# Top-32 sparse cross-attention: searching folded score halves, and building the weights from signs on the scalar engine

## The chip, the cores and the metric

The kernel runs on one core of a Trainium2 chip. The metric is the device time of one execution, in microseconds (us). A step or a tile below is 128 rows of scores: two heads of one batch element, 64 queries each.

## What is computed

The program is a perceiver of four layers, each with a cross-attention, a self-attention and a feed-forward part, on x of shape 16 x 64 x 128 with a context of shape 16 x 1601 x 128. The change concerns one part, the cross-attention of the last layer:

```
scores = jnp.einsum('bhsd,bhnd->bhsn', Q, K) / SCALE            # 16 x 16 x 64 x 1601
topk_scores, topk_indices = jax.lax.top_k(scores, 32)
sparse_weights = jax.nn.softmax(topk_scores, axis=-1)
context = sum over the 32 of sparse_weights * V[topk_indices]
x = x + context @ Wo.T + bo
```

Of each row of 1601 scores only the 32 largest get a weight.

## The kernel before

The stage is `stage_l3_xattn` (L1376); its last call, `cross_attention` (L322) with `topk` set, holds nearly all of its work. A tile t has 128 rows (two heads of a batch element) by 1601 scores, there are 8 tiles for each of 16 batch elements and so 128 in all. The tiles are written out 16 at a time (`iteration`): the first and the last 16 stand alone, the six groups between run in a hardware loop (`Fori`). Semaphores alone order the engines; each engine's own order is the order of its code.

What each engine does with a tile:

- TensorE: `scores` (L458) multiplies four banks of PSUM full (8 passes of 512 or fewer columns), two tiles ahead (`AHEAD`, L341). Once per batch element `project` (L477) makes the keys in the same PSUM tile `psS`. `turn` (L495) transposes the weights in 13 chunks through `psT`, `values` (L508) multiplies them with the context into `psU` (26 passes), `turn_u` (L517) and `sums` (L523) bring the heads together.
- ScalarE: `copy_scores` (L594) moves the scores from PSUM to `SS`; `stationary` (L575) the keys, once per batch element; `exps_topk` computes EX = exp(SS - max) (L600) and, once the search is over, ER = exp(rest - max) (L602), in which the 32 largest are gone; `copy_weights` (L612) copies the transposed chunks, four at a time; `norm` (L608) divides by the sum.
- VectorE: `maxima` (L718) searches. It finds the eight largest values (`max`, L731 and L737) and strikes them out (`match_replace`, L735 and L738), four times, each over all 1601 columns. Between them it negates the maximum (L732), inverts the sum of weights (`inverse`, L783) and copies the head outputs (`copy_ut`, L787). Once per batch element `add` adds the result (L793) and the bias (L794) to x.
- GpSimd (POOL): P = EX - ER (L701), and once per batch element the spread queries (L691).

The search of a tile, as VectorE runs it:

```
link(dve.max(top[:, 0, :], SS[:, k, :]))
dve.tensor_scalar(m, top[:, 0, 0:1], -1.0, None, ALU.mult).then_inc(max_ready, 1)
if between:
    between()
link(dve.match_replace(rest[:, k, :], top[:, 0, :], SS[:, k, :], -3.0e38))
for r in range(1, 4):
    link(dve.max(top[:, r, :], rest[:, k, :]))
    last = dve.match_replace(rest[:, k, :], top[:, r, :], rest[:, k, :], -3.0e38)
```

The loads of the context (SP queue, L421 to L424) are issued when the values of the batch element that used the buffer are done.

Of the kernel before, what the change touches and what calls it, by code (L numbers as in the profile page):

```python
# [5 lines left out]
ALU = mybir.AluOpType  # L6
ACT = mybir.ActivationFunctionType
# [7 lines left out]
B, S, D = 16, 64, 128  # L15
NT = B * S // 128
K = 1601
KC = [(c * 128, min(128, K - c * 128)) for c in range((K + 127) // 128)]
KB = [(c * 512, min(512, K - c * 512)) for c in range((K + 511) // 512)]
H = 16  # L20
# [6 lines left out]
ONE = 1  # L27
# [74 lines left out]
def bc(ap, shape):  # L102
    return ap.to_broadcast(shape)
# [1269 lines left out]
                         None, 0.125, False)  # L1373


def stage_l3_xattn(c):  # L1376

    nc, d = c.nc, c.dram
    layernorm(c)
    with ExitStack() as st:  # L1380
        N = c.sb(st, "N3", [128, H, D])
        QT = c.sb(st, "QT", [128, B * S])
        WT = c.sb(st, "WT", [128, 3, D])
        bias = c.sb(st, "biases", [128, 3])
        with ExitStack() as s2:
# [11 lines left out]

            spread_bias(c, bias[:, 2:3], WT[:, 2, :], bo)
            project(c, QT, WT[:, 0, :], c.xnT, bias[:, 0:1], 8.0 ** -0.5)
        cross_attention(c, None, N, None, topk=(QT, WT[:, 1, :], bias[:, 1:2]))  # L1400


def spread_bias(c, col, w, bo):
# [1426 lines left out]
def add_aligned(c, hi_dram, lo_dram):  # L2830
# [4 lines left out]
    with ExitStack() as st:  # L2835
# [12 lines left out]
        with nc.Block() as block:  # L2848
# [68 lines left out]

STAGES = [stage_l0_xattn, stage_l0_attn, stage_l0_ffn, stage_l1_xattn, stage_l1_attn, stage_l1_ffn, stage_l2_xattn,
          stage_l2_attn, stage_l2_ffn, stage_l3_xattn, stage_l3_attn, stage_l3_ffn]


# [34 lines left out]
```

## Time and profile before

| what | value |
|---|---|
| median of 3 runs | 6238.86 us (6229.23 to 6241.07) |
| the profiled execution's own time | 6232.65 us |
| its span | 6230.8 us |
| mean granted TensorE clock, share of full | 0.801 |
| busy: TensorE, VectorE, ScalarE, GpSimd | 4076.0, 4351.5, 2261.9, 937.9 us |
| the stage that is changed, from its first projection to its last add | 3667.55 to 5787.18 us of the span |

Times in the rows below are microseconds from the start of the span; PE is TensorE's matmul side, DVE is VectorE, ACT is ScalarE, POOL is GpSimd. In a row of a group, "x384" is the number of instructions, then comes their busy time and the mean of one in nanoseconds, then the idle time before them and what ended it. In a row of the timeline the first number is the start, the second how long the row's instructions took together; brackets hold the idle time before them and its releaser.

### The profile page before, as it was taken

The numbers are of one execution on the slowest core, as the hardware profiler recorded it, in microseconds if no ns is written. First come the engines' busy times: TensorE is split into PE (matmuls) and PEld (weight loads), VectorE is DVE, ScalarE is ACT, GpSimd is POOL, SyncE is SP. The second block draws the span as 40 slices with busy tenths as digits, with TensorE's granted clock in tenths as the row PEclk, the third lists the DMA queues.
The fourth block names the chain that finished last, engine by engine and source line by source line (L and its number), as shares of the span: only waits on it lengthen the run. The fifth ranks groups of instructions, "written<-read, shape, count | busy, mean of one in ns | idle before, by whom it ended". The sixth has DMA issues, their size and how long they took to land. (4 is left out here: it accounts for less than half of the span.)

```text
span 6230.8 us, 69499 instructions
## 1 busy us (share of the span) xinstructions
PE 4076.0 (65%) x23936; PEld 3283.5 (53%) x23936; DVE 4351.5 (70%) x5857; ACT 2261.9 (36%) x3210; POOL 937.9 (15%) x537
## 2 busy tenths in 40 slices
PE   4511556259999856799997546666666666666475
PEld 3201523148888834688886324454444545445464
DVE  3486334667777642577775369999999999999343
ACT  0000012126666532466664214444444444444111
POOL 1200010011111010212110102222222222222100
PEclk7755567679999978999998778887888887878676
DMA  6643300011111000111100000000000000000000
GB/s 209 154 109 81 91 2 0 4 46 33 33 33 33 12 6 27 47 37 33 38 28 13 4 24 11 11 11 22 11 11 11 11 22 11 11 11 1 15 0 12
DMA packets 199464, 198.78 MB, mean 32 GB/s; under 512 B 10908, under 2 KB 182124, under 8 KB 199164
## 3 DMA queue, kind: packets, MB, share of 16 engines
q1 hardware_dynamic: 179132, 156.79, 9.1%
q10 hardware_dynamic: 20032, 38.13, 2.1%
q8 instruction: 172, 2.82, 0.2%
q14 instruction: 128, 1.05, 0.1%
HBM read 161.47 MB, written 33.42 MB: 31 GB/s over the span
## 5 line engine op out<-in xcount | busy, mean ns | idle before, releaser
L1127 PEld LDWEIGHTS psU<-ctxN,ST 128*128 128x128 f32 x6656 | 859.5, 192 | 71.0 <-issue 9.5
L1127 PE MATMUL psU<-ctxN,ST 128*128 128x129 f32 x6656 | 869.1, 276 | 4.4 <-issue 4.4
L495 PE MATMUL psT<-ident,P 128*128 128x128 f32 (+1 forms) x1664 | 366.3, 376 | 600.9 <-POOL P L701 564.2
L737 DVE MAX8 top<-rest 128x8 f32<-128x1601 f32 x384 | 702.3, 1829 | 37.3 <-DVE rest L738 2.7
L738 DVE MATCH_REPLACE8 rest<-top,rest 128x1601 f32<-128x1601 f32 x384 | 695.4, 1811 | 0.0
L701 POOL TENSOR_TENSOR P<-EX,ER 128x1601 f32<-128x1601 f32 x128 | 457.7, 3576 | 1463.9 <-ACT ER L602 1463.9
L495 PEld LDWEIGHTS psT<-ident,P 128*128 128x128 f32 (+1 forms) x1664 | 275.5, 195 | 643.6 <-issue 420.6
L1213 ACT ACTIVATE ST<-ST 128x512 f32<-128x512 f32 (+1 forms) x832 | 519.8, 626 | 219.4 <-DVE ST L1316 216.6
L1316 DVE TENSOR_TENSOR ST<-ST,psB 128x512 f32<-128x512 f32 (+1 forms) x832 | 561.8, 678 | 13.4 <-PE psB L1146 13.4
L1302 DVE TENSOR_TENSOR psA<-psA,ST 128x512 f32<-128x512 f32 x640 | 445.5, 696 | 131.3 <-ACT ST L1205 68.8
L458 PE MATMUL psS<-KT,stat 128*128 128x512 f32 (+1 forms) x1024 | 438.9, 577 | 88.2 <-ACT KT L575 73.9
L508 PE MATMUL psU<-ctxN,PT 128*128 128x129 f32 (+1 forms) x3328 | 480.5, 304 | 0.0
L508 PEld LDWEIGHTS psU<-ctxN,PT 128*128 128x128 f32 (+1 forms) x3328 | 471.2, 223 | 0.0
L612 ACT ACTIVATE PT<-psT 128x512 f32<-128x512 f32 (+1 forms) x512 | 260.2, 516 | 492.1 <-PE psT L495 492.0
L1115 PE MATMUL psS<-statL,ctxH 128*128 128x512 f32 x832 | 395.1, 475 | 6.2 <-ACT ST L1205 2.7
L458 PEld LDWEIGHTS psS<-KT,stat 128*128 128x128 f32 x1024 | 210.1, 216 | 315.7 <-issue 236.1
L602 ACT ACTIVATE ER<-rest,mx 128x1601 f32<-128x1601 f32 x128 | 208.8, 1631 | 417.8 <-DVE rest L738 417.8
L1205 ACT ACTIVATE ST<-psS,key_bias 128x512 f32<-128x512 f32 (+1 forms) x416 | 284.1, 683 | 146.3 <-PE psS L1115 144.5
L1115 PE MATMUL psS<-statH,ctxH 128*128 128x512 f32 x832 | 331.6, 399 | 0.0
L1115 PE MATMUL psS<-statH,ctxL 128*128 128x512 f32 x832 | 328.6, 395 | 0.0
L1208 ACT ACTIVATE ST<-psS 128x512 f32<-128x512 f32 (+1 forms) x416 | 246.6, 593 | 158.9 <-PE psS L1115 156.2
L594 ACT ACTIVATE SS<-psS 128x1601 f32<-128x1601 f32 x128 | 192.1, 1501 | 207.3 <-PE psS L458 207.0
(420 smaller groups left out, 6690.5 us busy)
## 6 DMA issues: line engine op xcount, KB each, us to landing
ctxT<-ctxT_scratch SPq DMA_DIRECT2D x64, 800.5 KB, 4.3
ctxN<-in_ctx SPq DMA_DIRECT2D x64, 768.0 KB
ctxT_scratch<-ctx_trn ACTq DMA_DIRECT2D x16, 800.5 KB, 7.4
ctx_nat<-in_ctx SPq DMA_DIRECT2D x16, 768.0 KB
dist_scratch<-dd ACTq DMA_DIRECT2D x8, 800.5 KB, 5.4
cur<-cost_scratch SPq DMA_DIRECT2D x16, 400.2 KB, 6.7
left<-cost_scratch SPq DMA_DIRECT2D x16, 400.2 KB, 7.8
step_scratch<-nxt ACTq DMA_DIRECT2D x8, 800.5 KB, 3.4
```

The source lines that it names most:

```text
L458: last = pe.matmul(psS[:, o:o + w], stat[:, j, 2 * n:2 * n + 2, :], KT[:, j, o:o + w], start=True, stop=True)
L495: last = pe.transpose(psT[0:w, q % 2, (k % 4) * 128:(k % 4) * 128 + 128], P[:, t % 2, o:o + w], c.ident[:])
L508: last = pe.matmul(psU[:, 0:VW], PT[0:w, t % 2, k, :], ctxN[0:w, t // TB, k, 0:VW], start=(k == 0), stop=(k == len(KC) - 1))
L701: pool.tensor_tensor(P[:, t % 2, :], EX[:], ER[:], ALU.subtract).then_inc(p_ready, 1)
L737: link(dve.max(top[:, r, :], rest[:, k, :]))
L738: last = dve.match_replace(rest[:, k, :], top[:, r, :], rest[:, k, :], -3.0e38)
L1115: last = pe.matmul(psS[:, i % RING, :], x[:, u // 2 % 2, o:o + 128], q[:, p % 2, heads, queries], start=(n_pass == 0), stop=(n_pass == 2))
L1127: last = pe.matmul(psU[:, q, 0:D + 1], ST[0:n, i % SLOTS, q * 128:q * 128 + 128], ctxN[0:n, j, k, 0:D + 1], start=(k == 0 and q % 2 == 0), ...
L1205: act.activation(ST[0:n, i % SLOTS, :], psS[0:n, i % RING, :], ACT.Identity, bias=key_bias[0:n, col:col + 1]).then_inc(copied, 1)
L1213: act.activation(ST[0:n, i % SLOTS, :], ST[0:n, i % SLOTS, :], ACT.Exp).then_inc(exp_done, 1)
L1302: dve.tensor_tensor(psA[:], psA[:], cell, ALU.max).then_inc(folded, 1)
L1316: dve.tensor_tensor(cell, cell, psB[0:n, :], ALU.subtract).then_inc(shifted, 1)
```

## The change

`stage_l3_xattn` calls a new function, `topk_cross_attention`, in place of `cross_attention` with `topk` set. All 128 tiles are written out, with no hardware loop.

- Search: each row is folded into pairs. Columns 0 to 800, read from PSUM, and columns 801 to 1600, read from `SS` with one column of padding behind them, give an elementwise maximum and an elementwise minimum of 801 columns each, side by side in `pairs`. Two rounds of `max` and `match_replace` run over the maxima alone, the third over both halves, and the fourth is a `max` only: its eighth value is the 32nd score, the edge.
- Weights: ScalarE takes Sign(edge - score) over the row and over the 32 found values, with their sums. GpSimd and VectorE work out from the sums how many scores equal the edge and what share each of them gets. ScalarE turns the signs into a huge value above the edge, the share at it and nothing below (Relu), GpSimd clamps to 1 and multiplies with EX.
- Order: TensorE computes the scores one tile ahead of the search, and the projection stands right before the scores of a batch element's first tile. Transposes and values belong to the tile two steps back. The head outputs are copied by ScalarE, sums are made for two batch elements at once, and the bias is added once, by GpSimd, before the tiles.

The diff, cut to what matters here:

```diff
--- before.py
+++ after.py
+def topk_cross_attention(c, N, QT, WkT, bk):
+
+    nc = c.nc
+    NC = len(KC)
+    TB = H // 2
+    T = B * TB
+    HALF = (K + 1) // 2
+    KP = 2 * HALF
+    LOW = -3.0e38
+    STEEP = 1.0e28
+    TOPK = 32
+    LISTS = 7
...
+        SS = c.sb(st, "SS", [128, 3, KP])
+        pairs = c.sb(st, "pairs", [128, 2, KP])
+        EX = c.sb(st, "EX", [128, 2, K])
...
+                for j in range(3):
+                    pool.memset(SS[:, j, K:KP], LOW).then_inc(filled, 1)
+                pool.tensor_tensor(c.x[:], c.x[:], bc(c.bias_row[:].rearrange("p (a d) -> p a d", a=1), [128, NT, D]),
+                                   ALU.add).then_inc(filled, 1)
...
+                    if b >= 2:
+                        sp.wait_ge(u_ready, TB * (b - 1) + ONE)
...
+                def project(b):
+                    pe.wait_ge(loaded[b % 2], 48 * (b // 2 + 1) + ONE)
+                    if b:
+                        pe.wait_ge(copied, TB * b + ONE)
+                        pe.wait_ge(folded, 2 * TB * b + ONE)
+                    for o, w in KB:
+                        last = pe.matmul(psS[:, o:o + w], WkT, ctxT[:, b % 2, o:o + w], start=True, stop=True)
+                    last.then_inc(kp_ready, 1)
+
+                def scores(t):
+                    b, n = t // TB, t % TB
+                    if n == 0:
+                        project(b)
+                        pe.wait_ge(kt_ready, b + 1 + ONE)
+                        pe.wait_ge(stat_ready, b + 1 + ONE)
+                    else:
+                        pe.wait_ge(copied, t + ONE)
+                        pe.wait_ge(folded, 2 * t + ONE)
+                    for o, w in KB:
+                        last = pe.matmul(psS[:, o:o + w], stat[:, b % 2, 2 * n:2 * n + 2, :], KT[:, b % 2, o:o + w],
+                                         start=True, stop=True)
+                    last.then_inc(scored, 1)
...
+                scores(0)
+                for s in range(T + 2):
+                    if s + 1 < T:
+                        scores(s + 1)
+                    t = s - 2
+                    if t >= 1:
+                        turn_u(t - 1)
+                        if t % (2 * TB) == 0:
+                            sums(t // (2 * TB) - 1)
+                    if t >= 0:
+                        turn(t, 0)
+                        turn(t, 1)
+                        values(t, 0)
+                        turn(t, 2)
+                        values(t, 1)
+                        turn(t, 3)
+                        values(t, 2)
+                        values(t, 3)
+                turn_u(T - 1)
+                sums(NT - 1)
...
+                def keys(b):
+                    act.wait_ge(kp_ready, b + 1 + ONE)
+                    if b >= 2:
+                        act.wait_ge(scored, TB * (b - 1) + ONE)
+                    act.activation(KT[:, b % 2, :], psS[:, 0:K], ACT.Identity, bias=bk).then_inc(kt_ready, 1)
+                def copy_scores(t):
+                    if t % TB == 0:
+                        keys(t // TB)
+                    act.wait_ge(scored, t + 1 + ONE)
+                    if t >= 3:
+                        act.wait_ge(sided, t - 2 + ONE)
+                        act.wait_ge(exp_done, t - 2 + ONE)
+                    act.activation(SS[:, t % 3, 0:K], psS[:, 0:K], ACT.Copy).then_inc(copied, 1)
...
+                    act.activation(mneg[:, t % 2:t % 2 + 1], top[:, t % 2, 0:1], ACT.Copy, scale=-1.0
+                                   ).then_inc(max_ready, 1)
...
+                    act.activation(EX[:, t % 2, :], SS[:, t % 3, 0:K], ACT.Exp, bias=mneg[:, t % 2:t % 2 + 1]
+                                   ).then_inc(exp_done, 1)
...
+                def count_sides(t):
+                    j = t % 2
+                    edge = top[:, j, TOPK - 1:TOPK]
+                    act.wait_ge(listed, LISTS * (t + 1) + ONE)
+                    if t:
+                        act.wait_ge(marked, t + ONE)
+                    if t >= 2:
+                        act.wait_ge(spanned, 2 * (t - 1) + ONE)
+                        act.wait_ge(share_ready, t - 1 + ONE)
+                    act.activation(sides[:], SS[:, t % 3, 0:K], ACT.Sign, scale=-1.0, bias=edge,
+                                   accum_out=below[:, j:j + 1]).then_inc(sided, 1)
+                    if t:
+                        act.wait_ge(counted, t + ONE)
+                    act.activation(listed_sides[:], top[:, j, :], ACT.Sign, scale=-1.0, bias=edge,
+                                   accum_out=above[:, j:j + 1]).then_inc(counted, 1)
...
+                    act.wait_ge(share_ready, t + 1 + ONE)
+                    act.wait_ge(sided, t + 1 + ONE)
+                    if t >= 2:
+                        act.wait_ge(turned, 4 * (t - 1) + ONE)
+                    act.activation(P[:, j, :], sides[:], ACT.Relu, scale=-STEEP, bias=share[:, j:j + 1]
+                                   ).then_inc(marked, 1)
...
+                copy_scores(0)
+                for s in range(T + 2):
+                    if 0 <= s - 1 < T:
+                        count_sides(s - 1)
+                    if s + 1 < T:
+                        copy_scores(s + 1)
+                    if 0 <= s - 1 < T:
+                        mark(s - 1)
+                    if s < T:
+                        negate(s)
+                        exps(s)
+                    if s >= 3:
+                        copy_ut(s - 3)
+                    if s >= 2:
+                        for q in range(4):
+                            copy_weights(s - 2, q)
+                        norm(s - 2)
...
+                def equal_span(t):
+                    j = t % 2
+                    pool.wait_ge(counted, t + 1 + ONE)
+                    pool.wait_ge(sided, t + 1 + ONE)
+                    if t >= 2:
+                        pool.wait_ge(span_inverted, t - 1 + ONE)
+                    pool.tensor_scalar(span[:, j:j + 1], above[:, j:j + 1], 2.0, below[:, j:j + 1], ALU.mult, ALU.subtract
+                                       ).then_inc(spanned, 1)
+                    pool.wait_ge(spanned, 2 * t + 1 + ONE)
+                    pool.tensor_scalar(span[:, j:j + 1], span[:, j:j + 1], float(K), None, ALU.add
+                                       ).then_inc(spanned, 1)
+
+                def weigh(t):
+                    j = t % 2
+                    pool.wait_ge(span_inverted, t + 1 + ONE)
+                    if t >= 2:
+                        pool.wait_ge(marked, t - 1 + ONE)
+                    pool.tensor_scalar(share[:, j:j + 1], above[:, j:j + 1], float(TOPK), inv_span[:, j:j + 1],
+                                       ALU.add, ALU.mult).then_inc(share_ready, 1)
+                    pool.wait_ge(marked, t + 1 + ONE)
+                    pool.tensor_scalar(P[:, j, :], P[:, j, :], 1.0, None, ALU.min).then_inc(clamped, 1)
+                    pool.wait_ge(clamped, t + 1 + ONE)
+                    pool.wait_ge(exp_done, t + 1 + ONE)
+                    pool.tensor_tensor(P[:, j, :], P[:, j, :], EX[:, j, :], ALU.mult).then_inc(p_ready, 1)
...
+                def fold(t, low):
+                    j = t % 2
+                    lo, hi = psS[:, 0:HALF], SS[:, t % 3, HALF:KP]
+                    dve.wait_ge(copied, t + 1 + ONE)
+                    if t >= 2:
+                        dve.wait_ge(listed, LISTS * (t - 1) + ONE)
+                    if low:
+                        dve.tensor_tensor(pairs[:, j, HALF:KP], lo, hi, ALU.min).then_inc(folded, 1)
+                    else:
+                        dve.tensor_tensor(pairs[:, j, 0:HALF], lo, hi, ALU.max).then_inc(folded, 1)
...
+                    dve.max(top[:, j, 8 * n:8 * n + 8], pairs[:, j, 0:width]).then_inc(listed, 1)
...
+                    dve.match_replace(pairs[:, j, 0:width], top[:, j, 8 * n:8 * n + 8], pairs[:, j, 0:width], LOW
+                                      ).then_inc(listed, 1)
...
+                def invert_span(t):
+                    j = t % 2
+                    dve.wait_ge(spanned, 2 * t + 2 + ONE)
+                    if t >= 2:
+                        dve.wait_ge(share_ready, t - 1 + ONE)
+                    dve.reciprocal(inv_span[:, j:j + 1], span[:, j:j + 1]).then_inc(span_inverted, 1)
+
+                def inverse(t):
+                    dve.wait_ge(u_ready, t + 1 + ONE)
+                    if t >= 2:
+                        dve.wait_ge(us_ready, t - 1 + ONE)
+                    dve.reciprocal(li[:, t % 2:t % 2 + 1], psU[:, D:D + 1]).then_inc(li_ready, 1)
+
+                def add(p):
+                    dve.wait_ge(y_ready, p + 1 + ONE)
+                    dve.tensor_tensor(c.x[:, p, :], c.x[:, p, :], psZ[:, 128:256], ALU.add).then_inc(y_added, 1)
+
+                fold(0, False)
+                fold(0, True)
+                for s in range(T + 2):
+                    if s < T:
+                        find(s, 0, HALF)
+                    if s >= 3:
+                        inverse(s - 3)
+                    if s < T:
+                        drop(s, 0, HALF)
+                        find(s, 1, HALF)
+                    if 0 <= s - 1 < T:
+                        invert_span(s - 1)
+                    if s < T:
+                        drop(s, 1, HALF)
+                        find(s, 2, KP)
+                    if s - 2 > 0 and (s - 2) % (2 * TB) == 0 and s - 2 < T:
+                        add((s - 2) // (2 * TB) - 1)
+                    if s + 1 < T:
+                        fold(s + 1, False)
+                    if s < T:
+                        drop(s, 2, KP)
+                    if s + 1 < T:
+                        fold(s + 1, True)
+                    if s < T:
+                        find(s, 3, KP)
+                inverse(T - 1)
+                add(NT - 1)
...
 
             spread_bias(c, bias[:, 2:3], WT[:, 2, :], bo)
             project(c, QT, WT[:, 0, :], c.xnT, bias[:, 0:1], 8.0 ** -0.5)
-        cross_attention(c, None, N, None, topk=(QT, WT[:, 1, :], bias[:, 1:2]))
+        topk_cross_attention(c, N, QT, WT[:, 1, :], bias[:, 1:2])
 
 
 def spread_bias(c, col, w, bo):
```

## Rows read from the trace of the kernel before

**Rows 1.** Timeline, PE and DVE: the first projection and the last add of the stage.
```profile
3667.55 5.81 PE L477 MATMUL psS<-ctxT,WT 128*128 128x512 f32 x8 [11.20 <-DMA ctxN<-in_ctx]
...
5786.89 0.29 DVE L794 TENSOR_TENSOR x<-x,bias_row 64x128 f32<-64x128 f32 x1
```

**Rows 2.** Windows of the stage: busy time of each engine, granted clock, DMA share, GB/s.
```profile
3800.00:4056.00 256.00, 164.73 (x845) 127.32 (x845) 247.59 (x245) 113.20 (x131) 61.00 (x18) 0.83 0.04 13
```

**Rows 3.** Groups of instructions in the stage, VectorE.
```profile
L737 DVE MAX8 top<-rest 128x8 f32<-128x1601 f32 x384 | 702.3, 1829 | 37.3 <-DVE rest L738 2.7 <-DVE rest L735 2.7
L738 DVE MATCH_REPLACE8 rest<-top,rest 128x1601 f32<-128x1601 f32 x384 | 695.4, 1811 | 0.0
...
L738 DVE MATCH_VALUE_LOAD rest<-top,rest 128x8 f32 x384 | 35.4, 92 | 35.2 <-DVE top L737 2.7
```

**Rows 4.** Timeline, VectorE: the start of a tile's small work, two tiles of the written-out end.
```profile
5740.01 0.15 DVE L732 TENSOR_SCALAR mx<-top 128x1 f32<-128x1 f32 x1
...
5755.38 0.15 DVE L732 TENSOR_SCALAR mx<-top 128x1 f32<-128x1 f32 x1
```

**Rows 5.** Groups by form, VectorE: a two-input operation from PSUM and from SBUF.
```profile
L1302 DVE TENSOR_TENSOR psA<-psA,ST 128x512 f32<-128x512 f32 x640 | 445.5, 696 | 131.3 <-ACT ST L1205 68.8 <-ACT ST L1208 58.6
...
L2688 DVE TENSOR_TENSOR a<-cur,left 128x1601 f32<-128x1601 f32 x8 | 14.6, 1829 | 0.8
```

**Rows 6.** Timeline, POOL and DVE: the two adds to x beside a POOL operation.
```profile
4773.44 3.56 POOL L701 TENSOR_TENSOR P<-EX,ER 128x1601 f32<-128x1601 f32 x1 [13.93 <-ACT ER L602]
...
4773.90 0.29 DVE L793 TENSOR_TENSOR x<-x,psZ 64x128 f32 x1
4774.30 2.85 DVE L794 TENSOR_TENSOR x<-x,bias_row 64x128 f32 x1
```

**Rows 7.** Groups by form, GpSimd.
```profile
L701 POOL TENSOR_TENSOR P<-EX,ER 128x1601 f32<-128x1601 f32 x128 | 457.7, 3576 | 1463.9 <-ACT ER L602 1463.9
...
L1244 POOL CAST ctxH<-ctxM 128x1601 fp32r<-128x1601 f32 x32 | 48.9, 1529 | 1027.1 <-DVE ctxM L1275 1027.1
...
L1255 POOL CAST statH<-statM 128x512 fp32r<-128x512 f32 x64 | 40.5, 633 | 107.6 <-DVE statM L1283 107.6
...
L1478 POOL TENSOR_SCALAR_AFFINE_SELECT flag<-flag 128x1 f32<-128x1 f32 x64 | 11.8, 185 | 4.4
```

**Rows 8.** Groups by form, ScalarE.
```profile
L612 ACT ACTIVATE PT<-psT 128x512 f32<-128x512 f32 x384 | 225.2, 597 | 384.2 <-PE psT L495 384.1
...
L600 ACT ACTIVATE EX<-SS,mx 128x1601 f32<-128x1601 f32 x128 | 207.4, 1621 | 1.2 <-issue 1.1
L594 ACT ACTIVATE SS<-psS 128x1601 f32<-128x1601 f32 x128 | 192.1, 1501 | 207.3 <-PE psS L458 207.0
...
L608 ACT ACTIVATE U<-psU,li 128x128 f32<-128x128 f32 x128 | 47.0, 367 | 74.5 <-DVE li L783 74.0 <-issue 0.5
...
L575 ACT ACTIVATE KT<-psS,biases 128x1601 f32<-128x1601 f32 x16 | 25.4, 1590 | 44.4 <-PE psS L477 44.4
```

**Rows 9.** Timeline, PE: two tiles and a projection between them.
```profile
4797.14 2.91 PE L495 MATMUL psT<-ident,P 128*128 128x128 f32 x12 [5.57 <-POOL P L701]
4799.85 1.93 PE L508 MATMUL psU<-ctxN,PT 128*128 128x129 f32 x8
...
4804.57 2.91 PE L477 MATMUL psS<-ctxT,WT 128*128 128x512 f32 x8
4811.68 5.54 PE L458 MATMUL psS<-KT,stat 128*128 128x512 f32 x8 [4.20 <-ACT KT L575]
...
4820.79 2.17 PE L508 MATMUL psU<-ctxN,PT 128*128 128x129 f32 x18
```

**Rows 10.** Windows, PE alone, of that stretch: busy, granted clock, DMA share, GB/s.
```profile
4798.00:4802.00 4.00, 4.00 (x20) 0.50 0.00 0
4803.00:4807.00 4.00, 4.00 (x21) 0.98 0.00 0
```

**Rows 11.** Groups by form, ScalarE: the table load of the stage.
```profile
L600 ACT ACT_TABLE_LOAD x1 | 1.3, 1283 | 0.0
```

158 lines of the change are left out of this document (added).

## The prediction

> **What bounds the kernel now.** I read four views. First the timeline at the stage's two ends [rows 1]: from the first projection at 3667.55 to the last add's end at 5787.18 it takes 2119.6 us, 16.56 us for each of 128 tiles. Then the windows [rows 2]: in 256 us VectorE is busy 247.6, TensorE 164.7, ScalarE 113.2, POOL 61.0. VectorE is the bound. Then the groups [rows 3]: each of a tile's four rounds costs 1.83 (max) + 0.09 (value load) + 1.81 (replace), 14.9 us together. Last the timeline of VectorE [rows 4]: where the tiles are written out, one takes 15.37, so all else costs 0.45 there. The loop's bounds, the projection and the adds to x make up the difference to 16.56.
>
> **The change, part by part.**
>
> *VectorE's own work.* A two-input operation costs 0.696 for 512 columns with one input in PSUM and 1.829 for 1601 in SBUF [rows 5], so 1.04 ns a column, and 1.00 for a fold of 801. For max and replace over 801 columns there is no row. Bounds: no shorter than now (1.83, 1.81), or shorter by 800 x 1.04 = 0.83. I take the second, because their present times are those of the 1.829 row, which does follow its columns. A tile is then: max 2 x 1.00 + 2 x 1.83, replace 2 x (0.98 + 0.09) + 1.90, folds 2 x 1.00, two small inversions at 0.15 [rows 4], gaps 0.3: 12.3 us, three less than 15.37. The fourth replace is gone, the copy of head outputs has moved to ScalarE. The bias adds of 2.85 [rows 6], one per batch element, leave too; their one successor on POOL, ahead of the tiles, costs 1024/1601 of 3.58 [rows 7], 2.3, on the path.
>
> *What queues behind what.* Three engines now wait for each other inside a step. Take step s from the end of values of tile s-3. VectorE inverts the sum of s-3 (in its queue behind the first max of s). ScalarE waits for it with its whole queue: norm 0.37, Sign over 1601 columns 1.63 (as the Exp with a bias, [rows 8]), Sign over 32 columns about 0.3, and two sums out; no row has such a sum, I bound it by 0 and 0.3 and take 0.2. That is 2.6 us. Meanwhile TensorE, whose scores of s+1 stand behind the values of s-3, needs 2.91 for them at full clock [rows 9] (the projection has the same eight passes). So copying the scores starts at 3.15. The Sign work is covered by TensorE, with 0.5 to spare.
>
> *The small hand-over.* After the signs: POOL, POOL, VectorE (reciprocal), POOL, then ScalarE's mark. No row has POOL's tensor_scalar on one column. Bounds: 0.185 (a select on one column) and 0.633 (a cast of 512) [rows 7]. I take 0.25, the one-column row plus a little for the pointers. With 0.1 a crossing, the share is there at about 4.0 and the score copy ends at 4.3, so 0.3 is left before it costs. VectorE's reciprocal stands between two rounds of the search and VectorE waits there 1.3 us per step: 12.3 + 1.3 = 13.7 is VectorE's ring, counted in inversion again.
>
> *The ring through ScalarE and TensorE.* scores 2.91; score copy 1.50, mark 1.63, negate 0.2, Exp 1.62, head copy 0.3, first weight copy 0.60, less 0.1 of overlap for each of four [rows 8]: 5.4; hand-overs 0.35 (estimate: 0.1 each, 0.15 more after a matmul; ends 0.1 and 0.5); then TensorE's tail behind the first weight copy: values, transposes, values, transpose, values, values. The tail depends on the clock. After its pause TensorE needs 1.93 for eight value passes and 2.91 for twelve transposes; later 18 passes take 2.17 [rows 9]. The granted clock is 0.50 in 4798 to 4802 and 0.98 in 4803 to 4807 [rows 10], that is 1.2 and 2.4 GHz, and it fell after TensorE had stood idle 5.57. The tail is 7.5 all slow, 3.75 all fast. In the new order TensorE does two groups of transposes and then stands about 5 us until the weight copy, like before, so I let it be slow for 3.9, the stretch at 0.50 that [rows 10] show: 3.9 + 0.48 x 3.75 = 5.7. Sum: 2.91 + 5.4 + 0.35 + 5.7 = 14.4, and 0.4 because one tile in some has slow scores (5.54 against 2.91, [rows 9]): **14.8 a tile**. That is over VectorE's 13.7, so VectorE waits at the inversion.
>
> *POOL.* Clamp between 1.53 (one-input cast) and 3.58 (two-input) [rows 7], I take 1.6, and the product 3.58. The mark ends 5.9 into the ring, so weights are there at 11.2. They are needed only behind the next scores: 3 us of cover, gone only if the ring fell below 11.
>
> *Per batch element.* The projection, before it hidden two tiles ahead, stands in the ring: 2.91 + keys 1.59 + hand-overs 0.35, and partly slow scores behind the short pause: 5.9 (ends 4.8 and 8), 15 times. For two batch elements at once 32 sums passes come ahead of the transposes: 3.9 at the value passes' fast rate, 7.7 slow; partly beside the Exp; I take 6 (ends 0 and 10), 7 times. Context loads wait on values of the batch before, with six tiles of cover; the SP queue loses nothing.
>
> *Sum.* 127 x 14.8 = 1880; 15 x 5.9 = 89; 7 x 6 = 42; filling until the first tile's values end 50; last sums 5: 2066 against 2119.6, that is -54, and +2 for the bias on POOL: -51. The profiled execution's own time is 6232.65, so 6181; the median lies 6.2 above it: **6188**.
>
> **Rivals.** A difference of 0.2% (12 us) is about what a measurement of this kernel can tell from none.
>
> 1. *The clock stays up and VectorE is the bound.* TensorE's order keeps it busier than before (its work per tile falls little, the tile gets shorter). With the tail at 3.75 the ring is 12.9 and VectorE's 13.7 rules: 127 x 13.7 + 15 x 5 + 55 = 1870, that is 5992. For it: only about 5 us of pause. Against: a pause of 5.57 was enough for 0.50 [rows 9, 10]. Chance 0.17.
> 2. *POOL's small operations are slow* (the slower side). Place: the three one-column operations in front of the mark. They decide from about 0.35 us each; at 0.63 it is 3 x 0.38 - 0.3 = 0.84 a tile, +107: 6295. For it: POOL's 0.633 for 512 columns and 1.529 for 1601 leave 0.21 without any column, and pointer operands come on top. Against: the select of 0.185. Chance 0.24.
> 3. *Table loads.* The stage now loads a table once, 1.28 us [rows 11]. If Sign and Relu don't lie with Exp, each tile gets two: 1.28 in the ring and 0.8 beyond the cover at the Sign, 2.1 x 127 = 267: 6455. For it: no row shows Sign beside Exp. Against: Copy, Identity and Exp alternate all through the stage with one load. Chance 0.07. The Trainium skill ("ScalarE: Activation LUTs", "Table sets: the hidden batching unit") says that one set is active at a time and that relu, copy, identity and abs come in every set; it doesn't name sign there. Its "What ACT_TABLE_LOAD costs" adds a drain of about 1.38 to each switch, by which this case would be an estimated 350 us dearer still.
> 4. *POOL holds the folds.* The add with both inputs in SBUF took 2.85 beside POOL's product, until that ended, and the one with an input in PSUM 0.29 in the same stretch [rows 6]. A fold has one input in PSUM, like the short one. If it were held like the long one, up to 2.5 each, VectorE's ring is about 17.2: +2.4 x 127, 6490. Chance 0.04. The Trainium skill ("SBUF — State Buffer", "Who interferes with whom") has two SBUF inputs, not one, as the condition; this trace agrees, 2.85 against 0.29.
> 5. *Max and replace don't shorten with their columns:* VectorE's ring 13.7 + 3.3 = 17.0, some 6470. Chance 0.02.
>
> **How the numbers follow.** The forecast has 0.46; its own range, with tail, batch and sum costs at their ends, is 6090 to 6270, so 0.38 of it is faster, 0.05 within 0.2% and 0.03 slower. Rival 1 is faster. Rival 2 begins at no change: 0.03 faster, 0.05 the same, 0.16 slower. Rivals 3 to 5 are slower. Faster 0.58, same 0.10, slower 0.32. The range 6030 to 6320 leaves out rivals 3 to 5 (0.13) and the far part of rival 1 (0.07).
>
> **What would show it.** Right: VectorE idle ahead of the inversion of the value sum, released by TensorE; a folded max near 1.00; folds near 1.00; tiles 14 to 15.5 apart and about 6 more at every eighth; a granted clock of 0.50 at the first value passes. Rival 1: no such wait and 13.7 apart. Rival 2: a one-column POOL operation of over 0.35, and mark released by POOL. Rival 3: 250 table loads. Rival 4: folds with a spread up to 3.5. The forecast is wrong if the score copy doesn't wait for the scores, or if the weight copies aren't what TensorE's values wait for.

## The result and the profile of the changed kernel

The changed kernel takes 6053.96 us (median of 4 runs, 6051.49 to 6061.95) against 6234.05 us (6228.55 to 6241.07) on the same chip: ratio 0.9711, 95% interval 0.9696 to 0.9725, so 180 us less. The prediction said 6188, 51 us less than the median of before that was known then (6238.86). The profiled execution took 6051.49, its span is 6049.8, and its mean granted clock 0.810 (0.801 before).

The ends of the stage, in the timelines of TensorE and VectorE, where before stand [rows 1]:

```profile
3668.20 4.79 PE L1463 MATMUL psS<-ctxT,WT 128*128 128x512 f32 x8 [13.24 <-DMA ctxN<-in_ctx]
...
5598.50 0.29 DVE L1730 TENSOR_TENSOR x<-x,psZ 128x128 f32<-128x128 f32 x1 [5.03 <-PE psZ L1513]
```

5598.79 - 3668.20 = 1930.6 us, 189.0 less than before. Behind the stage 451.0 us are left, 443.6 before: the other 7.4 us were given back there, in code that didn't change. So the question is one stage, and there one tile.

The groups of the stage (x128 is once a tile). Columns: number of instructions, busy us, mean ns, idle us before them and what ended it.

```profile
L1669 POOL TENSOR_SCALAR P<-P 128x1601 f32<-128x1601 f32 x128 | 552.1, 4314 | 333.7 <-ACT P L1591 333.7
L1672 POOL TENSOR_TENSOR P<-P,EX 128x1601 f32<-128x1601 f32 x128 | 457.8, 3577 | 10.7
...
L1578 ACT ACTIVATE sides<-SS,top 128x1601 f32<-128x1601 f32 x128 | 207.6, 1622 | 5.6 <-DVE top L1707 5.4
L1591 ACT ACTIVATE P<-sides,share 128x1601 f32<-128x1601 f32 x128 | 207.5, 1621 | 2.6 <-POOL share L1666 2.6
...
L1655 POOL TENSOR_SCALAR span<-above,below 128x1 f32<-128x1 f32 x128 | 39.2, 306 | 392.1 <-ACT listed_sides L1582 392.1
L1666 POOL TENSOR_SCALAR share<-above,inv_span 128x1 f32<-128x1 f32 x128 | 34.2, 268 | 38.5 <-DVE inv_span L1720 38.5
L1658 POOL TENSOR_SCALAR span<-span 128x1 f32<-128x1 f32 x128 | 29.2, 228 | 10.5
...
L1578 ACT ACTIVATION_READ_ACCUMULATOR sides<-SS,top 128x1 f32 x128 | 24.3, 190 | 0.0
...
L1726 DVE RECIPROCAL li<-psU 128x1 f32<-128x1 f32 x128 | 21.4, 168 | 222.4 <-PE psU L1497 222.4
L1720 DVE RECIPROCAL inv_span<-span 128x1 f32<-128x1 f32 x128 | 21.0, 164 | 140.0 <-POOL span L1658 140.0
L1566 ACT ACT_TABLE_LOAD x1 | 1.3, 1283 | 0.0
```

VectorE, by form:

```profile
L1707 DVE MAX8 top<-pairs 128x8 f32<-128x1602 f32 x256 | 467.2, 1825 | 4.4
L1707 DVE MAX8 top<-pairs 128x8 f32<-128x801 f32 x256 | 252.6, 987 | 4.4
L1712 DVE MATCH_REPLACE8 pairs<-top,pairs 128x801 f32<-128x801 f32 x256 | 250.4, 978 | 0.0
L1712 DVE MATCH_REPLACE8 pairs<-top,pairs 128x1602 f32<-128x1602 f32 x128 | 231.9, 1811 | 0.0
```

Max and replace follow their columns, the folds (L1691, L1693) take 0.98, Sign and Relu come without a table load of their own, POOL's one-column operations take 0.23 to 0.31, and VectorE now waits in two places of a plain tile, for the value sum and for the span. (A plain tile is any but the first two of a batch element, those in which head sums are made, and those right behind these.)

One plain tile, the timeline of all engines from one inversion of a value sum to the next (start, duration; brackets hold the idle time before it and its releaser):

```profile
4686.70 2.91 PE L1476 MATMUL psS<-KT,stat 128*128 128x512 f32 x8
4686.90 0.17 DVE L1726 RECIPROCAL li<-psU 128x1 f32<-128x1 f32 x1 [1.50 <-PE psU L1497]
...
4687.37 1.62 ACT L1578 ACTIVATE sides<-SS,top 128x1601 f32<-128x1601 f32 x1
...
4689.65 1.51 ACT L1553 ACTIVATE SS<-psS 128x1601 f32<-128x1601 f32 x1 [0.26 <-PE psS L1476]
...
4690.14 0.16 DVE L1720 RECIPROCAL inv_span<-span 128x1 f32<-128x1 f32 x1 [1.08 <-POOL span L1658]
...
4691.05 1.62 ACT L1591 ACTIVATE P<-sides,share 128x1601 f32<-128x1601 f32 x1
4691.29 1.83 DVE L1707 MAX8 top<-pairs 128x8 f32<-128x1602 f32 x1
...
4692.79 1.63 ACT L1566 ACTIVATE EX<-SS,mneg 128x1601 f32<-128x1601 f32 x1
4693.04 0.97 DVE L1693 TENSOR_TENSOR pairs<-psS,SS 128x801 f32<-128x801 f32 x1
...
4694.49 1.07 ACT L1600 ACTIVATE PT<-psT 128x512 f32<-128x512 f32 x2
4695.22 1.52 PE L1497 MATMUL psU<-ctxN,PT 128*128 128x129 f32 x8 [4.62 <-ACT PT L1600]
...
4697.38 1.93 PE L1497 MATMUL psU<-ctxN,PT 128*128 128x129 f32 x8
...
4699.27 1.28 PE L1497 MATMUL psU<-ctxN,PT 128*128 128x129 f32 x10
...
4700.39 1.88 PE L1476 MATMUL psS<-KT,stat 128*128 128x512 f32 x4
4700.59 0.17 DVE L1726 RECIPROCAL li<-psU 128x1 f32<-128x1 f32 x1 [1.25 <-PE psU L1497]
```

This is how a ring is read: each bracket names who was late. The scores take 2.91; the score copy starts 0.04 behind them; ScalarE's row of work runs without a gap from 4689.65 until TensorE's values start at 4695.22, 5.57; and TensorE's tail lasts until the next scores at 4700.39, 5.17. Together 13.69 us. VectorE's wait at the end of this tile is the 1.25 us of 4700.59, the same at every plain tile looked at; the 1.50 at 4686.90 ends the tile before, the one behind the head sums. The starts of L1726 through the whole stage show 13.69 at plain tiles, 19.6 at a batch element's first tile with 14.3 behind it, and 20.2 where the head sums are made, with 13.9 behind it. 127 x 13.69 = 1739, 15 x 6.5 = 98, 7 x 6.75 = 47, and some 47 for the first tile and the last sums: 1931.

### The profile page after: what moved, and what is told of

The parts are those of the page before. It is cut to its first block and busy times, and to the rows that moved or that the text cites. A ratio compares the mean times of both kernels' runs of the same rounds, so it can differ in the third digit from the quotient of the medians.

```text
span 6049.8 us, 68883 instructions
## 1 busy us (share of the span) xinstructions
PE 4024.5 (67%) x23680; PEld 3292.2 (54%) x23680; DVE 3812.9 (63%) x5705; ACT 2530.6 (42%) x3978; POOL 1595.2 (26%) x1053
## 5 line engine op out<-in xcount | busy, mean ns | idle before, releaser
L1497 PE MATMUL psU<-ctxN,PT 128*128 128x129 f32 (+1 forms) x3328 | 622.8, 352 | 565.9 <-ACT PT L1600 565.9
L1497 PEld LDWEIGHTS psU<-ctxN,PT 128*128 128x128 f32 (+1 forms) x3328 | 581.0, 262 | 592.6 <-issue 588.4
L1707 DVE MAX8 top<-pairs 128x8 f32<-128x801 f32 (+1 forms) x512 | 709.2, 1406 | 8.9
L1669 POOL TENSOR_SCALAR P<-P 128x1601 f32<-128x1601 f32 x128 | 552.1, 4314 | 333.7 <-ACT P L1591 333.7
L1712 DVE MATCH_REPLACE8 pairs<-top,pairs 128x801 f32<-128x801 f32 (+1 forms) x384 | 482.2, 1256 | 0.0
L1672 POOL TENSOR_TENSOR P<-P,EX 128x1601 f32<-128x1601 f32 x128 | 457.8, 3577 | 10.7
L1476 PE MATMUL psS<-KT,stat 128*128 128x512 f32 (+1 forms) x1024 | 379.9, 513 | 42.2 <-ACT KT L1544 27.0
L1244 POOL CAST ctxH<-ctxM 128x1601 fp32r<-128x1601 f32 x32 | 49.0, 1531 | 1028.7 <-DVE ctxM L1275 1028.7
L1476 PEld LDWEIGHTS psS<-KT,stat 128*128 128x128 f32 x1024 | 185.7, 191 | 232.8 <-issue 203.6
L1487 PE MATMUL psT<-ident,P 128*128 128x128 f32 (+1 forms) x1664 | 308.0, 320 | 0.4 <-POOL P L1672 0.4
```

What stands on the lines that cost most here:

```text
L1476: last = pe.matmul(psS[:, o:o + w], stat[:, b % 2, 2 * n:2 * n + 2, :], KT[:, b % 2, o:o + w], start=True, stop=True)
L1487: last = pe.transpose(psT[0:w, q % 2, (k % 4) * 128:(k % 4) * 128 + 128], P[:, t % 2, o:o + w], c.ident[:])
L1497: last = pe.matmul(psU[:, 0:D + 1], PT[0:w, t % 2, k, :], ctxN[0:w, t // TB % 2, k, 0:D + 1], start=(k == 0), stop=(k == NC - 1))
L1669: pool.tensor_scalar(P[:, j, :], P[:, j, :], 1.0, None, ALU.min).then_inc(clamped, 1)
L1672: pool.tensor_tensor(P[:, j, :], P[:, j, :], EX[:, j, :], ALU.mult).then_inc(p_ready, 1)
L1707: dve.max(top[:, j, 8 * n:8 * n + 8], pairs[:, j, 0:width]).then_inc(listed, 1)
```

## The experiments

Two theories stood against each other. **The ring theory**: scores, ScalarE and TensorE's tail close the tile, and VectorE waits. **The VectorE theory**: the prediction had VectorE's own ring, with its wait at the span, at 13.7 a tile, which is just the spacing found; by it the rest of the prediction's ring would be an error, and each microsecond of VectorE's work would count. All runs are timed against the kernel before on their chip (medians 6229.74, 6236.82 and 6235.01 for the three groups of runs).

**VectorE's work reduced.** The third round and the last maximum over the 801 maxima only (the minima are never searched, so a pair with two of the 32 scores gives one):

```diff
-                        find(s, 2, KP)
+                        find(s, 2, HALF)
...
-                        drop(s, 2, KP)
+                        drop(s, 2, HALF)
...
-                        find(s, 3, KP)
+                        find(s, 3, HALF)
```

> The third round and the last max search only the 801 maxima, so that the weights of some rows are not those of the reference. VectorE has 2.5 us less to do per tile. Theory A (a ring through ScalarE and TensorE sets the pace: scores, score copy, mark, Exp, weight copies, values, with 1.5 us in which VectorE waits at the inversion): nothing to gain, 6045 to 6060 us against 6054 of the changed kernel, and VectorE's wait at the inversion grows from 1.5 to about 4 us. Theory B (VectorE's own work sets the pace): 127 x 2.5 = 317 less, about 5740.

6057.21 us, ratio 0.9722 (0.9701 to 0.9743): no change. The work went out and the wait took its place, as this kernel's group of the stage shows:

```profile
L1726 DVE RECIPROCAL li<-psU 128x1 f32<-128x1 f32 x128 | 21.6, 168 | 519.1 <-PE psU L1497 518.7
```

518.7 - 222.4 = 296 us, 2.3 a tile. VectorE doesn't set the tile.

**The ring lengthened.** The mark is made twice, the first time into a tile that nobody reads:

```diff
+        again = c.sb(st, "again", [128, 2, K])
...
+                    act.activation(again[:, j, :], sides[:], ACT.Relu, scale=-STEEP, bias=share[:, j:j + 1])
                     act.activation(P[:, j, :], sides[:], ACT.Relu, scale=-STEEP, bias=share[:, j:j + 1]
```

> The mark (Relu) is computed twice, once into a spare tile: 1.53 us more on ScalarE per tile, nothing on VectorE, TensorE or POOL. Theory A (ring through ScalarE and TensorE): the ring grows by 1.53 and more of the values fall into a low clock, 127 x 1.53 = 194 or more: 6250 to 6320 us. Theory B (VectorE's work is the bound, ScalarE has slack): no change, 6054.

6258.4 us, ratio 1.0048 (1.0031 to 1.0066): 204 us more, where 127 x 1.62 = 206 is what the second mark takes on ScalarE. In the profiled execution (6272.95, the longest of the five) the stage is 230 us longer and what lies behind it 8 us shorter. So ScalarE's large passes count in full, and TensorE's tail adds to them: its pause is 6.13 us in place of 4.62, the tail behind it takes 4.9 to 6.5 us in place of 5.17, and the spacing is no longer even (14.9 to 16.6, 1.9 more in the mean).

**VectorE's work increased.** All rounds over 1602 columns:

```diff
-                        dve.wait_ge(folded, 2 * t + 1 + ONE)
+                        dve.wait_ge(folded, 2 * t + 2 + ONE)
...
-                        find(s, 0, HALF)
+                        find(s, 0, KP)
...
-                        drop(s, 0, HALF)
-                        find(s, 1, HALF)
+                        drop(s, 0, KP)
+                        find(s, 1, KP)
...
-                        drop(s, 1, HALF)
+                        drop(s, 1, KP)
```

> All rounds of the search run over the full 1602 columns, as before the change, but with the new order and the sign weights. VectorE's ring grows by 3.3 us from 12.2 to 15.5 per tile. Theory A: 1.5 of it is covered by the wait at the inversion, the rest of 1.8 costs 127 x 1.8 = 230: about 6285 to 6310. So the halves would be worth 230 us, not 420. Theory B (VectorE has no slack): 127 x 3.3 = 420, about 6475.

6145.92 us, ratio 0.9861 (0.9841 to 0.9881): 92 us more, far below what was expected. The expectation counted only the wait at the value sum as cover. This kernel's groups show that the wait at the span went too:

```profile
L1724 DVE RECIPROCAL li<-psU 128x1 f32<-128x1 f32 x125 | 19.7, 157 | 48.2 <-PE psU L1497 48.2
L1718 DVE RECIPROCAL inv_span<-span 128x1 f32<-128x1 f32 x127 | 18.4, 145 | 0.0
```

Cover was 1.25 + 1.08 = 2.33 of the 3.33 us added, which leaves 1.0. Plain tiles take 14.57 to 14.63 and about every third 15.1, against 13.69, and in the profiled executions the stage is 115 us longer than the changed kernel's. Behind it, in code that didn't change, 23 us less are left, so that the whole is only some 95 longer. So VectorE bounds the tile only with some 2.3 us more work, and its own work of a plain tile is 14.6 - 3.33 = 11.3 us. Seen from the other side, searching half of the columns in the first two rounds brings 92 of the change's 180 us; the rest is the new order, the missing fourth replacement and the weights from signs together, which no run takes apart.

**The two moves that shorten the ring.** ScalarE's negation and exponential go behind the second weight copy, so that TensorE's tail starts while the exponential runs; VectorE inverts the span after its second replacement:

```diff
-                    if s < T:
-                        negate(s)
-                        exps(s)
                     if s >= 3:
                         copy_ut(s - 3)
                     if s >= 2:
-                        for q in range(4):
-                            copy_weights(s - 2, q)
+                        copy_weights(s - 2, 0)
+                        copy_weights(s - 2, 1)
+                    if s < T:
+                        negate(s)
+                        exps(s)
+                    if s >= 2:
+                        copy_weights(s - 2, 2)
+                        copy_weights(s - 2, 3)
                         norm(s - 2)
...
-                    if 0 <= s - 1 < T:
-                        invert_span(s - 1)
-                    if s < T:
                         drop(s, 1, HALF)
+                    if 0 <= s - 1 < T:
+                        invert_span(s - 1)
+                    if s < T:
                         find(s, 2, KP)
```

> Negation and Exp move behind the second weight copy on ScalarE, into the time in which it waits for the next transposes, and VectorE's inversion of the span moves one instruction back. Theory A: the ring loses 1.8 us, VectorE's ring of about 12 becomes the bound; 1.0 to 1.5 us less a tile, 130 to 190 in all: 5865 to 5925 us. Theory B (VectorE bound before the move): only the wait of 1.08 at the span goes, 127 x 1 = 130, and the wait at the inversion stays as it is. If neither holds, no change.

5778.2 us (5761.67 to 5799.22), ratio 0.9265 (0.9235 to 0.9295): 276 us less than the changed kernel, far more than the 130 to 190 that were expected. Then each move alone, with the clamp left out as a third:

> Of the two moves that were tried together (278 us less than the changed kernel), this is the first alone: ScalarE's negation and exponential (0.19 + 1.63 us of a tile) are issued after the first two of the four weight copies instead of ahead of them. Theory of the ring (a tile of 13.69 us is closed by scores, ScalarE and TensorE's values): the first values start about 1.8 us earlier in each tile, VectorE's wait for them (1.50 us at the inversion of the value sum) goes, and its wait for the span (1.08 us) stays, so a plain tile takes 13.69 - 1.50 = 12.2 us at best: up to 190 us less than the changed kernel's 6054, ratio to the kernel before 0.94 to 0.95. If the exponential's later end holds the weights of the tile after next instead, only some 40 us less, ratio 0.965. Theory that VectorE's own work bounds the tile: nothing, ratio 0.971.

> The second move alone: VectorE inverts the span (the row's divisor) after its second replacement instead of ahead of it. The wait of 1.08 us for POOL's span goes from VectorE. Theory of the ring through ScalarE and TensorE: the time that VectorE wins is waited out at the inversion of the value sum (1.50 us becomes about 2.6), and nothing is won: 6054 within 10, ratio 0.971. Theory that VectorE with its waits sets the tile: 1.08 us x 127 = 137 us less, ratio 0.949.

The first alone: 5834.05 us, ratio 0.9355 (0.9340 to 0.9371), 220 us less. Its fastest and most common plain tiles take 12.33 us, near the 12.2 expected. 195 us of the 223 between the two profiled spans lie in the stage; the other 27, which the expectation didn't have, lie behind it, in unchanged code, where the profile shows a granted clock of 0.72 and 0.79 in the first two stretches of 200 us against 0.65 and 0.72. The second alone: 6057.65 us, ratio 0.9714 (0.9698 to 0.9731), nothing. The wait only changes its place:

```profile
4688.75 0.16 DVE L1720 RECIPROCAL inv_span<-span 128x1 f32<-128x1 f32 x1
...
4699.20 0.17 DVE L1726 RECIPROCAL li<-psU 128x1 f32<-128x1 f32 x1 [2.33 <-PE psU L1497]
```

It pays only behind the first: once the ring is short enough, the span's 1.0 us is on the path (12.33 - 1.0 = 11.3, and with both together the fastest plain tiles take 11.28). 0 + 220 is less than 276: the gains don't add, because the bound passes from one ring to the other. The stages of the profiled executions say the same: 0 and 195 us alone, 263 together. Both kernels with the late exponential leave TensorE a pause of 2.87 us in many tiles, and the tail behind such a pause took 3.85, 5.0, 5.17 or 6.45 us; what decides which, these runs don't show.

**POOL's clamp left out.** Scores above the edge then weigh 1e28 against the share of those at it:

```diff
-                    pool.tensor_scalar(P[:, j, :], P[:, j, :], 1.0, None, ALU.min).then_inc(clamped, 1)
-                    pool.wait_ge(clamped, t + 1 + ONE)
```

> Leaves out POOL's minimum with 1 over the marks (4.31 us of a tile); the weights of the scores above the edge then come out too large, everything else is computed. POOL's work of a tile falls from 4.31 + 3.58 + 2.34 + 0.8 = 11.0 to 6.7 us. Theory of the ring: POOL ends its product long before the transposes want it, so nothing changes: 6054 within 10, ratio 0.971. Rival: POOL's clamp holds the product and with it the transposes, or its traffic slows VectorE's reads of SBUF: up to 4.3 x 127 us less on the path, or some 0.1 to 0.5 us of a tile (13 to 60 us) from faster searches.

6052.68 us, ratio 0.9704 (0.9687 to 0.9720): nothing. The clamp's 4.31 us a tile are off the path and don't slow VectorE either: the folds take 0.98 in both kernels, beside the clamp in the changed one and, for the first fold of a tile, beside the product here.

**TensorE kept busy in its pause.**

```diff
                         turn(t, 1)
+                        for _ in range(15):
+                            pe.matmul(psU[:, 256:384], c.ident[:], c.ident[:], start=True, stop=True)
                         values(t, 0)
```

> Adds 15 matmuls of 128x128 of the identity, into a part of the value bank that is unused then, in TensorE's pause of 4.6 us between the transposes of the second half and the values of the first. Nothing else is changed. Theory of the ring: the granted clock stays at its upper level through the tail of values and transposes (5.17 us of which 3.4 us are at the lower one), the tail takes about 1.3 us less of a tile, of which the waits that are left let 0.6 to 1.1 through: some 80 us less than the changed kernel, 5975, ratio 0.959 (0.950 to 0.965). Rival one: the clock's fall in the tail doesn't come from the pause, and the dummies only stand in the way: 0 to 40 us more. Rival two (VectorE bounds): nothing.

5846.43 us, ratio 0.9372 (0.9356 to 0.9388): 208 us less, where 80 were expected. The expectation put the 15 matmuls at 1.8 us; the trace shows them as 30 passes that take 3.51. The pause shrinks from 4.62 to between 1.3 and 2.0 us and the tail to 3.52:

```profile
4509.95 3.51 PE L1530 MATMUL psU<-ident 128*128 128x128 f32 x30
4515.02 1.13 PE L1497 MATMUL psU<-ctxN,PT 128*128 128x129 f32 x8 [1.55 <-ACT PT L1602]
...
4516.42 1.06 PE L1497 MATMUL psU<-ctxN,PT 128*128 128x129 f32 x8
...
4517.42 1.28 PE L1497 MATMUL psU<-ctxN,PT 128*128 128x129 f32 x10
4518.54 2.91 PE L1463 MATMUL psS<-ctxT,WT 128*128 128x512 f32 x8
```

The windows of TensorE alone say why; first this kernel's tails, then those of the changed kernel (first a batch element's first tile, behind the projection; then the plain tile above). Columns: us, busy, granted clock, DMA share, GB/s.

```profile
4502.70:4506.20 3.50, 3.50 (x31) 1.00 0.00 0
4515.00:4518.50 3.50, 3.48 (x31) 1.00 0.00 0
```

```profile
4502.10:4503.90 1.80, 1.80 (x8) 0.50 0.00 0
4503.90:4506.40 2.50, 2.50 (x13) 0.50 0.00 0
```

```profile
4695.20:4696.50 1.30, 1.28 (x8) 0.73 0.00 0
4696.50:4697.40 0.90, 0.90 (x7) 0.50 0.00 0
4697.40:4699.20 1.80, 1.80 (x10) 0.50 0.00 0
4699.30:4700.30 1.00, 1.00 (x12) 1.00 0.00 0
```

A value of 1.00 is 2.4 GHz and 0.50 is 1.2 GHz. In the plain tile the clock is still up when TensorE resumes after 4.62 us without work, falls to 0.50 during the first eight value passes and is up again for the last ten. With work in the pause it stays up. The changed kernel has the same case of its own: where head sums are made TensorE has 32 more passes to do and stands idle for only 0.34 us before the values, and that tail takes 3.52 too. With the 15 matmuls the tail gets 1.65 us shorter; VectorE's wait for the value sum (1.25) goes, and VectorE's own work with its wait at the span (1.0) then sets the tile: 12.33, 1.36 less. My expectation of 0.6 to 1.1 took too little of this. A batch element's first two tiles won more (16.3 and 12.35 instead of 19.6 and 14.3), the sums' tiles lost (21.5 instead of 20.2). The stage is 181.5 us shorter, and 22 us more were won behind it.

**A smaller dose.** 4 matmuls in place of 15:

```diff
-                        for _ in range(15):
+                        for _ in range(4):
```

> As the run with 15 matmuls in TensorE's pause, which took 208 us from the changed kernel, with 4 instead of 15 (some 0.5 us instead of 1.8 us of the 4.6 us pause). The theory that the tail is slow because TensorE idles ahead of it, with the pause nearly as long as before: most of the gain goes, 6040 (6000 to 6060), ratio 0.969. Rival, that any work at that place holds the clock: about the same gain as with 15, 5850, ratio 0.937.

6033.25 us, ratio 0.9683 (0.9652 to 0.9713). Plain tiles still take 13.69. The 4 matmuls take 1.06 us, the pause is 3.72, and the tail behind it, from the first values to the next scores, is 5.17 as before:

```profile
4698.92 1.71 PE L1497 MATMUL psU<-ctxN,PT 128*128 128x129 f32 x8 [3.72 <-ACT PT L1602]
...
4704.09 2.91 PE L1476 MATMUL psS<-KT,stat 128*128 128x512 f32 x8
```

So that some work stands at that place isn't enough. The interval overlaps that of the changed kernel; the stage is 23 us shorter in the profiled executions, nearly all of it at the first two tiles of a batch element and around the sums.

**The best version.** Both moves and the loop of matmuls with `range(9)`; and then this kernel without them in the sums' tiles and with `add` behind `find(s, 3, KP)`, whose diff against the one with 9 is:

```diff
-                        for _ in range(9):
+                        for _ in range(9 if t % (2 * TB) or not t else 0):
...
-                    if s - 2 > 0 and (s - 2) % (2 * TB) == 0 and s - 2 < T:
-                        add((s - 2) // (2 * TB) - 1)
...
                         find(s, 3, KP)
+                    if s - 2 > 0 and (s - 2) % (2 * TB) == 0 and s - 2 < T:
+                        add((s - 2) // (2 * TB) - 1)
```

> Both moves (5778 together) and 9 matmuls of the identity in the pause that is left to TensorE (2.87 us of a tile). Theory: with both moves VectorE's own work of 11.28 us bounds a plain tile wherever the tail runs at the upper clock, and the tiles of 11.6 to 13.6 us are those with a slow tail; held up, all plain tiles take 11.28 us. 127 x 11.28 = 1433, + 15 x 4.3 for the batch elements' first tiles, + 7 x 8 for the sums (as with the 15 matmuls) = 1554 against the 1614 us of both moves: 5718, ratio 0.917 (0.910 to 0.924). Rival: the clock is up often enough already and the 9 matmuls (1.05 us) only push the values back: 0 to 40 us more than both moves, ratio 0.927 to 0.934.

> As the last run, but without the 9 matmuls in the seven tiles in which the head sums are made, and with VectorE's addition of a sum after the last maximum of its tile instead of ahead of the first fold. Theory: VectorE's wait for the sum (7.44 us of each such tile with the 15 matmuls) and the push of 1.05 us go, the tile keeps a hold-up of 2 to 4 us because the transposes start 4.6 us late behind the sum's 32 matmuls: 7 x 3 to 7 x 5 = 20 to 35 us less than the run before it. Rival: the hold-up comes through the transposes alone and the addition waits beside it: 0 to 8 us less.

5726.33 us, ratio 0.9186 (0.9159 to 0.9214), 8 us off the expectation, most plain tiles at 11.29, the tile behind the sums at 13.0; and 5706.46 us, ratio 0.9163 (0.9128 to 0.9197). Between the two the intervals overlap, so the last 20 us aren't settled; the spacing shows 1.0 to 1.2 us less at six of the seven sums' tiles (16.1 to 16.4 for 17.3 to 17.6), some 7 us, and more of the batch elements' first tiles at 14.9 instead of 16.6, which nothing in the edit aims at. Both beat the kernel before and the changed one, the latter by 328 and 348 us.

## Why the prediction was wrong in its size

The mechanism was right, the size was not: 51 us less were forecast, 180 came. The ring through ScalarE and TensorE bounds the tile, as forecast, and VectorE waits at the inversion. The prediction's 14.8 came out as 13.69; the difference of 1.1 x 127 = 140 us is the error (135 in the stage as a whole). 6054 lies below the 6090 to 6270 that the prediction gave this mechanism, and within its whole range of 6030 to 6320 only by the room left for the first rival, which is luck. Of its signs for being right, tiles 14 to 15.5 apart didn't come, and the clock wasn't yet at 0.50 when a plain tile's values began. By its terms:

- *The Sign work ahead of the score copy.* 2.6 predicted with 0.5 to spare; it takes 2.28 and 0.26 are left. Off the path, as forecast.
- *Scores and ScalarE.* 2.91 and 5.4 predicted; 2.91 measured, and of the 5.57 from the score copy to the values 5.4 is ScalarE's own row. Right, and the doubled mark shows that they count in full.
- *Hand-overs 0.35.* 0.04 at the score copy, and 0.13 to the values: 0.17. 0.18 too much.
- *Tail 5.7.* **This is the step that failed most**: I let the tail be slow for 3.9 us from its first pass on, by [rows 10]. Measured are 5.17. The all-fast tail is 3.52, not 3.75, which is 0.23 of the difference; and the clock fell only during the first value passes, so that the slow stretch is 2 x (5.17 - 3.52) = 3.3 us long and not 3.9, which is the other 0.30. Together 0.53 too much. The run with TensorE kept busy shows that the clock is what the rest of the tail's length depends on.
- *Slow scores 0.4.* None in plain tiles: all eight passes at 2.91. 0.4 too much. The slow scores of [rows 9] stood behind the projection's pause; I spread them over all tiles although the batch term held them already.
- *VectorE's ring 13.7.* Its sum with the wait agrees with the measured spacing by chance. Measured: 11.3 of own work and a wait of 1.0, 12.33 in the run with the late exponential and in the one with 15 matmuls. Of the 12.3 for own work the maxima, replacements and folds were right to 0.1; the 0.3 of gaps was wrong in sign, since consecutive rows overlap by up to 0.1 each (1.83 from 4691.29, the next at 4693.04).
- *POOL.* The three small operations: 0.25 each predicted, 0.31, 0.23 and 0.27 measured; the mark follows the score copy at once and waited for the share 2.6 us in the whole stage. The clamp was put at 1.6 within 1.53 to 3.58 and took 4.31, outside both bounds. It cost nothing, as its absence shows, but the cover said to be 3 us is smaller than thought: the product ends at 4700.7 and the transposes start behind the next scores, some 2.5 us later.
- *Batch element 5.9, sums 6.* Measured 5.9 at the first tile, whose tail is slow from its first pass (the windows at 4502.10 above) and takes 6.43, and 0.6 at the next, whose tail takes 5.80; 6.5 for the sums and 0.2 for the tile behind them.
- *The fill and the last sums, 55:* about 47.

The rivals. The first (clock up, VectorE the bound) isn't what happened, as the clock fell in the tail and a plain tile took 13.69 by the other ring; but its core, that the clock decides how long the tail is, holds, and the run with 15 matmuls is this rival made real, with 5846 us in place of its 5992, since VectorE's ring was 12.33 and not 13.7. The second: no small operation over 0.32. The third: one table load in the stage; the Trainium skill ("ScalarE: Activation LUTs", "Table sets: the hidden batching unit") doesn't name sign among the functions of a set, and this trace shows that Sign, Relu, Exp, Copy and Identity alternate for 128 tiles with a single load of 1.28 us. The fourth: the folds take 0.98 with the clamp beside them, and 0.98 beside the product in the kernel without the clamp. The fifth: 0.987 and 0.978 for 801 columns.

What stays open: why the rest of the kernel behind the stage takes 424 to 458 us from version to version. The clock granted there differs, but no run changed it alone. It adds to or takes from what a run shows by up to 27 us, so the stages are compared beside the medians above.

## What to carry to other kernels

When several engines wait for each other in turn, write the ring out as one sum, and then a second sum for every other ring; the one that is longest hides all edits to the others (taking 2.5 us of VectorE's work out of a tile bought nothing, and an edit worth nothing alone was worth 56 us behind another). In such a ring look first for work that stands ahead of a hand-over without being needed by it: moving one exponential behind two copies was worth more than the whole change. And where TensorE stands idle inside each turn, read from the trace how much of its next work runs at the lower clock: a stretch taken over from another order of the code was part of the largest error here. Then try what keeping it busy gives.

## What the hardware showed that wasn't expected

- A `tensor_scalar` minimum over 128x1601 on GpSimd took 4.31 us, longer than the two-input product of the same size (3.58) and almost three times the cast of that size (1.53, [rows 7]). The Trainium skill ("GPSIMD Engine Reference", "Engine selection") has one-input work at roughly line rate there; these runs show otherwise for this operation.
- ScalarE's sum beside a function (`accum_out`) costs an instruction of its own, 0.19 us, whether 1601 or 32 columns were summed.
- An addition of matmuls in TensorE's pause, 3.51 us of useless work a tile, made the kernel 208 us faster; 1.06 us of it left the plain tiles as they were.
